# Three cross-attention layers: score copies in four places, another order of projection pairs, and keys stored by ScalarE

## The reference

```python
q = (x @ Wq + bq); k = (ctx @ Wk + bk); v = (ctx @ Wv + bv)     # L1, L2: no biases
scores = q @ k.T * scale                                          # per head
# L0: clip(scores, -10000, 10000); L2: where(mask, scores, -max)
out = softmax(scores) @ v @ Wo (+ bo)
x = x + out
```

## Time and profile before

| what | value |
|---|---|
| median of 3 runs | 3099.77 us (3097.92 to 3100.94) |
| the profiled execution | 3105.24 us, span 3103.5 us |
| clamped layer | scores from 308 us, to about 640 us |
| bare layer | about 1142 us to 1505 us |
| masked layer | about 1945 us to 2268 us |
| PE busy in the whole span | 84% |
| DVE, ACT, POOL busy | 47%, 42%, 29% |

### The profile page before, as it was taken

The page is one execution under the profiler, slowest core; times in us unless marked ns, Lnnn a source line. Parts: engine busy times, 40 slices in busy tenths (PEclk is TensorE's granted clock), DMA queues, the critical chain, the costliest instruction groups (busy, mean ns, idle before and its releaser), DMA issues. The chain is left out here.

```text
span 3103.5 us, 56465 instructions
## 1 busy us (share of the span) xinstructions
PE 2613.3 (84%) x18499; PEld 1924.0 (62%) x18500; DVE 1446.2 (47%) x3474; ACT 1289.6 (42%) x3858; POOL 890.6 (29%) x572
## 2 busy tenths in 40 slices
PE   5746899879777988998599877999959996989899
PEld 2345666656455555666489734666649995866566
DVE  5685888850544234444522376566550004654211
ACT  1334677742443123333223222677724342862211
POOL 3254455520001022222133244455522222430000
PEclk8867899979898999999899987999979998989899
DMA  2000000000142010000357600000045553013100
GB/s 104 1 1 27 20 16 20 15 30 1 40 107 66 0 44 16 20 15 15 124 192 238 211 33 33 21 20 19 11 186 186 180 184 100 1 43 89 40 14 24
DMA packets 108484, 194.45 MB, mean 63 GB/s; under 512 B 56276, under 2 KB 81060, under 8 KB 96596
## 3 DMA queue, kind: packets, MB, share of 16 engines
q1 hardware_dynamic: 93986, 166.93, 16.8%
q0 software_dynamic: 6816, 18.62, 2.0%
q10 hardware_dynamic: 7570, 7.47, 0.8%
HBM read 174.29 MB, written 18.71 MB: 62 GB/s over the span
## 5 line engine op out<-in xcount | busy, mean ns | idle before, releaser
L1353 POOL TENSOR_TENSOR L_xattn_p<-L_xattn_p,L_xattn_ri 112x1500 f32<-112x1500 f32 (+1 forms) x192 | 435.9, 2270 | 586.6 <-DVE L_xattn_ri L1661 586.6
L1566 ACT ACTIVATE L_xattn_pT<-ps 125x448 f32<-125x448 f32 (+1 forms) x576 | 255.8, 478 | 356.7 <-PE ps L1457 356.5
L1457 PEld LDWEIGHTS ps<-ident,L_xattn_p 112*125 112x125 f32 x1920 | 256.0, 191 | 100.5 <-issue 40.5
L1578 ACT ACTIVATE L_xattn_p<-L_xattn_sa,L_xattn_ng 112x375 f32<-112x375 f32 x512 | 305.1, 603 | 18.1 <-DVE L_xattn_ng L1677 10.4
L1457 PE MATMUL ps<-ident,L_xattn_p 112*125 112x112 f32 x1920 | 292.2, 284 | 9.5 <-POOL L_xattn_p L1353 4.9
L1009 PEld LDWEIGHTS ps<-L_ffn_xsT,L_ffn_w 128*128 128x128 f32 x2240 | 263.7, 194 | 7.0 <-issue 1.9
L1009 PE MATMUL ps<-L_ffn_xsT,L_ffn_w 128*128 128x128 f32 x2240 | 264.7, 277 | 2.4 <-ACT L_ffn_xsT L1039 2.4
L276 POOL TENSOR_TENSOR ln_rstd<-ln_tmp,half 112x8 f32<-112x8 f32 x26 | 44.3, 1719 | 701.2 <-DVE ln_tmp L225 525.1
L1479 PE MATMUL ps<-L_xattn_kT,L_xattn_qm 32*112 32x375 f32 (+1 forms) x1280 | 173.3, 523 | 70.1 <-DVE L_xattn_v L1604 21.4
L1071 DVE TENSOR_TENSOR L_ffn_y<-ps,L_ffn_pack 128x256 f32<-128x256 f32 x70 | 29.7, 425 | 364.6 <-PE ps L1018 364.6
L1018 PE MATMUL ps<-L_ffn_weights,L_ffn_hT 128*128 x840 | 193.5, 380 | 2.3 <-DVE L_ffn_hT L1083 2.3
(11 more groups left out here) (410 smaller groups left out, 5083.4 us busy)
## 6 DMA issues: line engine op xcount, KB each, us to landing
L_ffn_w<-in_L_ffn_experts SPq DMA_DIRECT2D x74, 1024.0 KB, 5.5
L_xattn_src<-in_ctx SPq DMA_DIRECT2D x48, 375.0 KB, 3.0
L_attn_toeplitz<-L_attn_h SPq DMA_DIRECT2D x4, 3136.0 KB, 23.1
L_ffn_weights<-in_L_ffn_experts SPq DMA_DIRECT2D x8, 1028.0 KB, 16.8
L_xattn_keys<-in_ctx SPq DMA_DIRECT2D x16, 281.2 KB, 6.0
L_xattn_rows<-in_ctx_rows SPq DMA_DIRECT2D x16, 281.2 KB
L_ffn_weights<-in_L_ffn_experts SPq DMA_DIRECT2D x8, 516.0 KB, 9.5
L_ffn_w<-in_L_ffn_experts SPq DMA_DIRECT2D x4, 1026.0 KB, 5.9
```

Of the source, the lines that this page charges most:

```text
L1353: g.tensor_tensor(P[:, m % 4, :, :], P[:, m % 4, :, :], ri[:, m % 4, :].unsqueeze(2).broadcast_to([T, W, S2]), ALU.mult).then_inc(s["prob_ ...
L1457: last = pe.transpose(turned(t)[:, j * T:(j + 1) * T], P[:, m % 4, j, kc * KW:(kc + 1) * KW], k.ident[0:T, 0:T])
L1566: act.activation(PT[:, m % 4, kc, :, :].rearrange("p h t -> p (h t)"), turned(t), ACT.Copy).then_inc(s["pt_ev_a"].sem, 1)
L1578: last = act.activation(P[:, m % 4, j, :], at, ACT.Exp, bias=ng[:, m % 4, j:j + 1], scale=-1.0 if mask else 1.0, accum_out=rs[:, m % 4, j: ...
```

## The change

It has four parts.

1. `sa` gets four places instead of two. The clip and the masked maxima then wait for the exponentials of unit n-4 and not of n-2. DVE's `share` moves: in the clamped layer behind the clip, in the masked layer between the two halves of the maxima. The masked layer gets a tiny copy (`pace`) that carries the wait.
2. In the bare layer a pair's large products come right behind its small ones, ahead of `weigh` and the transposes.
3. Keys are counted on a pair of signals of their own, `kt_mm` and `kt_ev`. The list in which places are looked up (`others`) no longer has keys, so `J_V2` is now 1; the flag `early` still reads `jobs[J_V2][3]`, and `jobs[1]` with W=4 is K.
4. In the clamped layer ACT stores the keys, as two activations with the bias, behind the first exponentials of the step at p=1. In the same layer V0 and V2 are now stored between the two maxima.

```diff
-    sa = sb("sa", [T, 2, W, S2]) if copied else None
+    sa = sb("sa", [T, 4, W, S2]) if copied else None
+    pace = sb("pace", [T, 1]) if mask else None
...
-    J = len(jobs)
-    names = [(kind, c) for kind, c, _, _ in jobs]
-    J_V0, J_V2, J_K, J_Q = (names.index(what) for what in (("V", 0), ("V", 2), ("K", 0), ("Q", 0)))
+    others = [what for what in jobs if what[0] != "K"]
+    names = [(kind, c) for kind, c, _, _ in others]
+    J, J_V0, J_V2, J_Q = len(others), names.index(("V", 0)), names.index(("V", 2)), names.index(("Q", 0))
...
@@ weigh
-                        last = isinstance(now, int) and now == B - 1
-                        pe.wait_ge(*job_out.at(counted(now, J_V0 if last else J_K)))
+                        pe.wait_ge(*job_out.at(counted(now, J_V0)))
+                        if not (isinstance(now, int) and now == B - 1):
+                            pe.wait_ge(*kt_ev.at(keys_ready(now + 1, 0)))
...
@@ PE, step
                 score(i, n)
                 if W == 2:
                     open_pair(i, n)
+                    close_pair(i, n)
                 weigh(i, n - OUT, first, b)
...
                 turn_over(i, n - TURN, (0, 1), first)
-                if W == 4 and not early:
+                if not early:
                     open_pair(i, n)
-                if W == 2 or not early:
                     close_pair(i, n)
...
@@ ACT
+            def keep_keys(i, n):
+                what = job_at(i, n, "K")
+                if not clamp or what is None:
+                    return
+                kind, c, b, u, count = what
+                act.wait_ge(*kt_mm.at(count))
+                act.wait_ge(*s["sc_mm"].at(b * UB))
+                for h in range(2):
+                    last = act.activation(KT[:, u, h, :], k.ps[:, job_bank(n) + h, 0:S2], ACT.Identity,
+                                          bias=pack["bk"][:, h:h + 1])
+                last.then_inc(kt_ev.sem, 1)
...
                 exponentials(i, n - LATE, (0,), first)
+                keep_keys(i, n)
                 store_turned(i, n - TURN, (2,), first)
...
@@ DVE, step
-                        v.wait_ge(*s["exp_done"].at(i * U + n - 1))
-                        v.tensor_scalar(sa[:, n % 2, :, :], scores(n), CLAMP, -CLAMP, ALU.min, ALU.max).then_inc(
+                        v.wait_ge(*s["exp_done"].at(i * U + n - 3))
+                        v.tensor_scalar(sa[:, n % 4, :, :], scores(n), CLAMP, -CLAMP, ALU.min, ALU.max).then_inc(
                             s["sc_read"].sem, 1)
-                if mask:
-                    share(i, n - 1 - LATE, first)
+                    elif mask:
+                        v.wait_ge(*s["exp_done"].at(i * U + n - 3))
+                        v.tensor_copy(pace[:, :], k.half[:, 0:1])
+                if clamp:
+                    share(i, n - 2, first)
                 if early:
                     keep(i, n, "KV")
...
-                maxima(i, n, range(HALVES))
+                maxima(i, n, (0,))
+                if mask:
+                    share(i, n - 2, first)
+                    maxima(i, n, (1,))
                 if not early:
                     keep(i, n, "KV")
+                if clamp:
+                    maxima(i, n, (1,))
```

More of the change, by code:

```diff
@@ L1280, in counted, with values_ready, queries_ready, keys_ready @@
         if isinstance(b, int) and b == B - 1:
-            return len(opening) + b * J + sum(1 for what in jobs[:j + 1] if what[2] == 0)
-        return len(opening) + b * J + j + 1
-    def ready(b, j):
-        if jobs[j][2] == 0:
-            return counted(b, j)
-        return len(opening) if isinstance(b, int) and b == 0 else counted(b - 1, j)
+            return 1 + b * J + sum(1 for what in others[:j + 1] if what[2] == 0)
+        return 1 + b * J + j + 1
+    def values_ready(b):
+        return counted(b, J_V2)
+    def queries_ready(b):
+        return 1 if isinstance(b, int) and b == 0 else counted(b - 1, J_Q)
+    def keys_ready(b, c):
+        return KS_ * b + c // 2 + 1
     def job_at(i, n, kinds):
         b, u, p = batch_of(i, n)
-        for j, (kind, c, off, step) in enumerate(jobs):
+        for kind, c, off, step in jobs:
             if step == p and kind in kinds and not (isinstance(b, int) and b + off >= B):
-                return kind, c, b, (1 - u if off else u), counted(b, j)
+                count = keys_ready(b + 1, c) if kind == "K" else counted(b, names.index((kind, c)))
+                return kind, c, b, (1 - u if off else u), count
         return None
@@ L1474, in score @@
                     if pair is not None:
-                        pe.wait_ge(*job_out.at(pair[4]))
+                        pe.wait_ge(*(kt_ev if pair[0] == "K" else job_out).at(pair[4]))
                 c, e, strips = heads(p)
@@ L1532, in _ @@
                     at += 2
-            pe.wait_ge(*job_out.at(len(opening)))
+            pe.wait_ge(*job_out.at(1))
+            pe.wait_ge(*kt_ev.at(KS_))
             stream(pe, step)
@@ L1633, in store @@
                         last = store_values(2, u, k.ps[0:KW, bank + h, cols], cols)
-                last.then_inc(job_out.sem, 1)
+                last.then_inc(kt_ev.sem if kind == "K" else job_out.sem, 1)
             def keep(i, n, kinds):
                 what = job_at(i, n, kinds)
-                if what is None:
+                if what is None or (clamp and what[0] == "K"):
                     return
                 kind, c, b, u, count = what
-                v.wait_ge(*job_mm.at(count))
+                v.wait_ge(*(kt_mm if kind == "K" else job_mm).at(count))
                 if kind == "V":
@@ L1668, in maxima @@
                 r = n % 4
-                at = sa[:, n % 2, :, :] if clamp else scores(n)
+                at = sa[:, n % 4, :, :] if clamp else scores(n)
                 for h in halves:
@@ L1682, in step @@
                 early = W == 4 and p == jobs[J_V2][3]
-                if not mask:
-                    share(i, n - 1 - LATE, first)
+                if not copied:
+                    share(i, n - 1, first)
                 if n < U:
@@ L1710, in _ @@
             at = 0
-            for j, (kind, c, off, p) in enumerate(opening):
-                v.wait_ge(*job_mm.at(j + 1))
+            for kind, c, off, p in opening:
+                v.wait_ge(*(job_mm.at(1) if kind == "Q" else kt_mm.at(c // 2 + 1)))
                 store(kind, c, 0, ONE if kind == "Q" else at)
```

29 lines of the change are left out of this document (18 added, 11 removed).

## The result

The changed kernel takes 3149.46 us (median of 4 runs, 3144.42 to 3153.12), the kernel before, beside it, 3100.36 us. The ratio is 1.0155, with a 95% interval of 1.014 to 1.017. The prediction was 3100 us with a range of 3083 to 3114, so the time lies 35 us above its upper end. The profiled execution took 3144.42 us with a span of 3142.6, which is 39.1 us more than the span before (3103.5). The medians differ by 49.1 us, and 10 of these stand in no trace: the changed kernel was profiled in the shortest of its four executions (granted clock of the whole span 0.916, against 0.912 and 0.913 in the others), and the kernel before in one that lies 5 us above its median.

What follows compares the result with a forecast made beforehand. PE was taken to bound all three layers. Masked +12.6, bare -12 and clamped 0 sum to +0.6 us on the profiled 3105.24; the median lies 5.5 us lower, giving 3100 us, range 3083 to 3114.

Steps and rivals of the forecast that it cites:

- Masked layer, given: Masked layer: score waits of 0.79 us at p=0 and 0.19 at p=3 go, together 0.98 us a batch.
- Masked layer, taken: Masked layer: scores of p=2 wait for maxima behind DVE's key copies, 1.82 us a batch lost.
- the clip's 0.81 us: Clamped layer, p=0: the scores' 0.81 us wait for the clip goes, as the clip no longer waits for exponentials.
- where I took 0.4: Clamped layer: transposes wait for POOL because `ri` comes behind the clip, between 0 and 0.8 us, taken as 0.4.
- the 1.6 us that it would have meant: Clamped layer: by the skill page's estimate of 1.09 us for two keys, the layer would be 1.6 us faster.
- where I had 0.84: Masked layer: net loss a batch, 1.82 - 0.98 = 0.84 us, times 15 is +12.6 us.
- The 0: Clamped layer: net of keys, clip and POOL, +0.4 - 0.81 + 0.4, so 0; ends -12 and +10 us.
- the clock of 0.99 to 1.00: All three layers: PE's granted clock in the steady part of the profile before, 0.99 to 1.00.
- The gains of 0.62 and 0.15 us: Bare layer: PE gains 0.62 us at p=1 and 0.15 at p=2 a batch, 9.9 and 2.2 us in all.
- the order changes nothing: Bare layer, p=1 and p=3: queries or output lie between, PE does not wait, so the order has no effect.
- some 29, 34 and 17 us: PE's idle time in the three layers over 16 batches, taken as the most an edit can win.
- The rival that named a limit for this layer (ScalarE needing 2.9 us): Bare layer: ACT needs 2.9 us, not 2.27, from transposes' load to exponentials' end; 0.62 us gone, 3112 us; chance 0.14.

Runs made afterwards that it cites:

- places_only: Kernel before with part 1 alone (four places for the score copies, new places of `ri`): 3093.35 us.
- keys_behind: Changed kernel with only DVE's `early` flag set to never, so keys and values are copied behind the maxima: 3112.22 us.
- filled_six: Changed kernel with six useless small PE products ahead of the masked layer's wait at p=2, from the third batch on: 3136.16 us.
- bare_order: Kernel before, bare layer only: order becomes small products, transposes 0 and 1, large products, `weigh`, transpose 2: 3073.08 us.
- combined: Changed kernel with PE's flag at p=2, DVE's never, `ri` earlier at two places, bare layer's transposes 0 and 1 ahead of the pair: 3060.94 us.
- both combined kernels: combined (3060.94 us), and the same kernel with the bare layer's order of bare_order (3038.95 us).
- both_flags: Changed kernel with `early` reading `others[J_V2][3]` on PE and DVE, so it marks p=2 again: 3089.27 us.
- flags_bare: both_flags with the bare layer's large products behind `weigh` and the transposes again, as in the kernel before: 3089.73 us.
- keys_dve: both_flags with DVE instead of ScalarE storing the clamped layer's keys, between its two maxima: 3087.99 us.
- the two filled kernels: Changed kernel with 14 or six useless small PE products ahead of the masked layer's wait at p=2: 3156.65 and 3136.16 us.

## Why the prediction was wrong

**What was right.** Most single waits came as walked.

- Masked layer, given: the scores of p=0 come 3.17 us after those of p=3 and not 4.03, and the wait of 0.19 at p=3 is gone.
- Masked layer, taken: the scores of p=2 come 6.30 us after those of p=1; 1.82 us later than before was forecast, 1.70 came.
- Clamped layer: the clip's 0.81 us went (4.08 to 3.17 from p=3 to p=0), and the stretch from p=0 to p=1 grew by 0.39 for POOL, where I took 0.4. The two keys took ScalarE 1.02 us, 0.56 each with an overlap of 0.10. I had taken 1.2, two exponentials (0.603 each) without an overlap. The estimate by the Trainium skill (ScalarE: Activation LUTs, What ACT_TABLE_LOAD costs) was 1.09 and nearer. Even so the layer did not gain the 1.6 us that it would have meant, it lost.
- Bare layer: the waits of the scores went, the exponentials ended 2.23 us behind the first load of the transposes, where I had 2.22, and the loads of the small products waited 0.68 us at p=1 where I had said 0.5.

**The first step that failed: V2's move had no price, and cost some 26 us.** The section on the change says that "at p=2 the V2 pair moved the other way", behind the transposes. The prediction walks only the key pair. The queries wait on the count of jobs for the one before them, V2, since both use the same bank. In the kernel before, two transposes lay between V2 and the queries and hid DVE's copy. Now the queries stand directly behind, and wait 0.60 us in the clamped and the masked layer. From p=2 to p=3 the batch grew from 6.74 to 7.70 and from 5.82 to 6.61 us. With it, the masked batch at full clock is 1.70 - 0.86 + 0.79 = +1.63, which is what was measured (19.73 to 21.37), where I had 0.84. The clamped batch got 0.66 longer, where I had 0: 0.95 from V2's move, 0.24 between p=1 and p=2, mostly because the third transposes now wait 0.20 us for ACT's copy of the first, less 0.53 for the clip's wait and POOL. The 0 was also wrong in the parts that were meant. In places_only the clamped batch is 1.15 us shorter, since the keys' wait goes with part 1, where I had credited that part with the clip's 0.81 us alone.

**The second: the wait was priced at its length, and the clock added some 14 us.** I took 1.82 us a batch for the maxima. Behind it the clock goes to its lower level. From keys_behind this is worth 14 of the 36 us that the key copies cost, and filled_six shows for the slow batches that PE's idle time at this place is the cause. For the layer's start no run shows it. The prediction took the clock of 0.99 to 1.00 of the earlier trace rows as given. That PE's new idle time could lower it was in no rival and no bound, and so the range was too narrow on the upper side.

**The third: groups of products were priced as long as in the old order, which cost some 7 us.** The gains of 0.62 and 0.15 us were worked out up to the small products of p=1 and p=3. There it came to 0.44 (7.60 to 7.16 us from the scores of p=0) and 0.06 (6.54 to 6.48 from those of p=2). The 0.18 us missing at p=1 is one term of that sum: I took 1.73 us for the large products, and in their new place they take 1.91. Where "the order changes nothing", from the small products of p=1 and p=3 to the next scores, it took 0.11 and 0.10 us more. So a batch gained 0.28 us and not 0.77. Behind it stands a premise that is right as an upper bound only: that PE's idle time, "some 29, 34 and 17 us", is what an edit can win. bare_order won 28.5 us of its 34, but in combined all waits of the bare layer are gone too and the batch is only 0.39 us shorter than before, since the groups of products themselves got longer. The rival that named a limit for this layer (ScalarE needing 2.9 us) is not what happened: the exponentials came when I thought.

In numbers for the steady batches: masked +24.5 instead of +12.6 at full clock (1.63 x 15), and 9 more for the six slow batches; clamped +9.9 instead of 0; bare -4.2 instead of -12. That is 39 us instead of 0.6. The layers' extents give 39.9. That they agree so well is in part luck: the low clock at the masked layer's start adds some 5 us, and the first batches of the masked and the clamped layer lost less than the steady ones, by about as much.

## What to carry to other kernels

When the order of two pieces of work is swapped, price what moved back as carefully as what moved ahead: ask of each job who waits for its result next, and what used to lie between the two. A bound engine's idle time is not a stock that an edit can draw on; compare the time from the start of a group to the start of the next one in both orders, since the order by itself changed it by 0.1 to 0.2 us a group here. And a new wait on PE can cost more than its length, because the clock may go down behind it: here the waits of 1.38 us brought another 9 us over the layer. Length alone does not decide it, as the next section shows, so look at the granted clock batch by batch.

## What the runs showed of the hardware

- A wait of 1.38 us in a batch of 21.4 us, with another of 0.60, took PE's clock down in every second batch of the masked layer, from 2.4 to 1.2 GHz for some 3.4 us. A wait of 0.62 us in keys_behind did not. With six useless products in the longer one, it stayed up. But waits of 1.28 and 0.89 us in a batch of 22.70 us (bare layer of the kernel before), and of 1.02 and 0.60 in one of 21.40 (clamped layer of the changed one), left the granted clock at 1.00. What tells these cases apart was not tested.
- The start of a layer differs too. The granted clock of the masked layer's first 22 us was 1.00 in before, keys_behind, bare_order and both combined kernels, 0.85 in both_flags, flags_bare, keys_dve and places_only, and 0.76 or 0.69 in the four kernels with the key copies ahead of the maxima. What in that stretch decides it I did not separate; the two filled kernels have the changed kernel's code in the first two batches, and gave 0.69 where it gave 0.76. Two kernels can differ there by 5 us (both_flags and keys_dve in the clamped layer), as much as the effects that one wants to measure. This is why steady batches are compared as well as extents.
- Four f32 products of 128 rows and 512 columns, from the start of the group to that of the next, took 1.73 us between transposes of 112 rows, 1.82 behind such transposes and ahead of `weigh` (bare_order), and 1.91 behind products of 64 rows and ahead of `weigh` (combined and the changed kernel). Each of the two neighbours accounts for 0.09 us.
- A product of 112 rows and 64 columns in f32, with its own load, took 0.21 us in a row of like ones (2.88 us for 14).
